# A fused recurrent and expert kernel: the experts' input turned and evicted by halves of the tokens, with scan units and LayerNorm steps moved between the stages

## The chip, the cores and the metric

One core of one Trainium2 chip. The metric is the device time of the whole kernel in microseconds. The kernel before was run three times: 2276.2 us is the median, 2268.3 the lowest and 2276.84 the highest. The kernel is written by engine: each of PE (TensorE), DVE (VectorE), ACT (ScalarE), POOL (GpSimd) and SP (which issues DMAs here) has its own list of instructions, and they meet at semaphores that the program counts itself.

## The reference, cut to what matters

```
x  = L0_attn_h                                  # (8, 512, 256)
xn = layernorm(x)
s  = minGRU-like scan over xn (two layers);  g = silu(expert layer of xn)
x  = x + s * g                                  # first half: phases a and b of the kernel
xn = layernorm(x)
s  = recurrent(xn)      # r,k,v,g,w from low-rank blends; state[i,j] = w[i]*state[i,j] + k[i]*v[j]; y = r . state
                        # 16 heads of 16 x 16; then LayerNorm over the head (ln_w, ln_b), * silu(g), @ oW.T
g  = silu(transformer block of xn):
        h   = xn + attention(rmsnorm(xn))       # 16 heads, latent kv of 32, rope on 32, causal
        hn  = rmsnorm(h) * w_ln2
        out = h + shared_expert(hn) + top-2 of 8 experts(hn)   # down(silu(gate) * up)
x  = x + s * g
```

The change touches the second half only (`phase_c`), which runs once for each of the 8 sequences of 512 tokens. All data are f32.

## The kernel before

`phase_c` (L963) takes the sequences one after another. Each engine runs `before_attention(0)`, `attention(0)`, and then seven times `experts(b)`, `before_attention(b + 1, b)`, `attention(b + 1)`, and at last `experts(7)`.

- **before_attention** (PE L1318, ACT L1552, DVE L1817, POOL L2060): the LoRA products `la_*` and `lb_*`; DVE blends them (L1821) into the mixes, to which POOL adds xn (L2064); projections `pr_*`; the turned input of attention; `ckv` and `q0` to `q7`. DVE's `rotate` (L1848) and POOL (L2079, L2082) apply rope. `sp0`, `sp1` give the bonus term, `lat` the latent values in token order (copied by ACT, L1578). The last steps of the sequence before (`ended`: LayerNorm of the second half of the heads, output product, residual) are woven in.
- **attention** (PE L1383, ACT L1580, DVE L1884, POOL L2084): 32 steps of one query tile and one pair of heads. Per step: `scores` on PE (L1238, L1241), row maximum on DVE (L1777), exp on ACT (L1587), `turn_probs` on PE (L1255), copy on ACT (L1596), and in every second group of four steps `weigh_values` (L1292). At its end the row normalization, the output product by tiles of 128 tokens (`wo0` to `wo3`, L1388), `add_rows` (L1908), `norm_rows` (L1914, L1917).
- **experts** (PE L1426, ACT L1637, DVE L1929, POOL L2105): the 512 normalized rows are turned (L1435), scaled and evicted (`xc0` by DVE, L1927; `xc1` by ACT, L1546), the routing product `gate` (128x8 pieces of L1375), top-two selection on DVE (L1941 to L1971), then nine experts in a row: `up` (two products of 128x512), silu on ACT, `hidden` on DVE (L1977), `down` (128x256 pieces), and DVE's weighted accumulation (L2011). The next sequence's head (L1683 to L1721, up to its `lerp`) is woven in by `between` (L1979).

The **scan units** run beside all this: the recurrence is done in `UNITS` = 32 units per sequence. For unit n SP brings broadcast values (`copy_value`), DVE does `outer(n)` (L1790) and `scan(n)` (L1797), POOL multiplies by r (`product`, L2058), and PE adds up four units (`reduce_state`, L1265) into bank 4 (`whole`). `AHEAD` = 4 units are scanned before attention's first step, those up to `STEPPED` = 22 are spread over the steps by `parts_by_step`, those up to `EARLY` = 24 follow in attention's tail, the rest stand in `experts`. There are 4 state buffers and 6 of products, so a scan waits for the product of four units before, and from the seventh on a product waits for a reduction. `read_out(b, m)` (L1807) takes the sum of 16 units; `mean_last`, `center_last` (L1743), POOL's square (L2116), `var_last` (L1307) and `root_last` (L1550) are the LayerNorm of the second half.

The order of work is written out by hand. `PRE` and `POST` name PE's outputs in order with the engine that reads each; `PRE_BANKS` and `POST_BANKS` give each one of seven PSUM banks, and before PE writes one it waits for the reader of the last output in that bank (`begin`, L1155). The semaphores count in the order of these tables.

## Time and profile before

| what | value |
|---|---|
| median of three runs | 2276.2 us |
| the profiled execution | 2276.78 us, span 2275.0 us from first to last instruction |
| mean granted TensorE clock | 0.963 of 2.4 GHz |
| busy, share of the span | PE 91%, DVE 79%, ACT 43%, POOL 37% |
| `phase_c` | from about 567 us to the end, eight sequences |
| DMA | 66 GB/s over the span |

Times in timelines are us from the span's start. A row of a timeline gives start, duration, engine, line, operation, output and input shapes and the number of merged instructions, and in brackets the engine's idle time before it with what ended it. An f32 product appears as two matmul records.

### The profile page before, as it was taken

Reading aid. Unit: us, or ns where it says so; the run is one execution under the profiler, and the core shown is the slowest. Engines: PE = TensorE matmul, PEld = TensorE weight load, DVE = VectorE, ACT = ScalarE, POOL = GpSimd, SP = SyncE. Lnnn points to the kernel's source line nnn. Section 1 sums busy time; section 2 is a strip of 40 time slices with the busy share of each in tenths; the row PEclk is TensorE's granted clock in tenths of the full one; section 3 lists DMA queues with packets and bytes.
Section 4 is the critical chain, followed back from the end, with each engine's and each line's share of the span. In section 5 each row is a group of like instructions: output and inputs, shape, how many; then the busy total and the mean of one; then the engine's idle time right before and its main releaser. Section 6 shows DMA issues by size and latency. Waiting matters only on the chain.

```text
span 2275.0 us, 37286 instructions
## 1 busy us (share of the span) xinstructions
PE 2062.7 (91%) x11722; PEld 1243.2 (55%) x11723; DVE 1794.2 (79%) x2906; ACT 974.1 (43%) x2556; POOL 846.5 (37%) x666
## 2 busy tenths in 40 slices
PE   7998599997988999998999889998989998899887
PEld 4554599997445445544554455455445544554554
DVE  5997466664697889779897988898798879887985
ACT  3444244442274237334623652373347235612741
POOL 1335200001543364336435542643364346326430
PEclk9999799998999999999999999999999999999998
DMA  6554411113222022211211230222122112302210
GB/s 174 145 158 138 146 54 54 52 55 116 64 57 80 1 65 71 61 37 47 66 47 47 61 86 4 61 66 70 29 56 66 47 47 57 79 15 60 61 48 10
DMA packets 145727, 151.18 MB, mean 66 GB/s; under 512 B 47664, under 2 KB 105648, under 8 KB 145584
## 3 DMA queue, kind: packets, MB, share of 16 engines
q1 hardware_dynamic: 138288, 136.73, 22.0%
q0 software_dynamic: 3072, 8.41, 1.1%
q10 hardware_dynamic: 4224, 4.19, 0.6%
q8 instruction: 83, 1.36, 0.3%
q14 instruction: 60, 0.49, 0.1%
HBM read 121.71 MB, written 27.43 MB: 66 GB/s over the span
## 4 chain that ended last, share of the span: by engine, by line
issue 24%; PE 23%; DVE 18%; POOL 8%; ACT 2%; DMA 0%; POOLq 0%; DVEq 0%; ACTq 0%
PE bank L1375 8%; PE bank L1238 4%; DVE arena L1777 4%; POOL arena L2064 3%; PE bank L1292 3%; DVE arena L1797 3%; DVE arena L1790 3%; PE bank L1255 3%; PE bank L1388 2%; POOL arena L2058 2%; DVE arena L2011 1%; ACT arena L1587 1%; POOL arena L2079 1%; PE bank L1265 1%; DVE arena L1852 1%
## 5 line engine op out<-in xcount | busy, mean ns | idle before, releaser
L2058 POOL TENSOR_TENSOR arena<-arena 128x512 f32<-128x512 f32 x256 | 337.1, 1319 | 567.9 <-DVE arena L1797 491.5
L1375 PE MATMUL bank<-arena 128*128 128x512 f32 (+2 forms) x1312 | 438.6, 489 | 6.8 <-DVE arena L1927 6.8
L1171 PE MATMUL bank<-arena 128*128 128x512 f32 (+2 forms) x768 | 360.5, 614 | 6.8 <-ACT arena L1542 5.4
L1797 DVE TENSOR_TENSOR_SCAN arena<-arena 128x512 f32<-128x512 f32 x256 | 361.9, 1414 | 1.7
L1587 ACT ACTIVATE arena<-bank,arena 128x128 f32<-128x128 f32 (+3 forms) x512 | 266.3, 531 | 194.9 <-DVE arena L1777 193.8
L1375 PEld LDWEIGHTS bank<-arena 128*128 128x128 f32 x1312 | 249.9, 203 | 177.2 <-issue 142.1
L1790 DVE TENSOR_TENSOR arena<-arena 128x512 f32<-128x512 f32 x256 | 249.0, 973 | 40.6 <-DMA arena<-values 36.5
L1238 PE MATMUL bank<-arena 64*128 64x128 f32 (+3 forms) x1024 | 207.5, 481 | 71.4 <-ACT arena L1587 49.7
L1171 PEld LDWEIGHTS bank<-arena 128*128 128x128 f32 (+2 forms) x768 | 139.5, 190 | 198.7 <-issue 171.5
L1777 DVE TENSOR_REDUCE arena<-bank 128x2 f32<-128x256 f32 (+3 forms) x256 | 206.9, 808 | 39.0 <-PE bank L1241 39.0
L1596 ACT ACTIVATE arena<-bank 128x128 f32<-128x128 f32 (+3 forms) x512 | 196.4, 441 | 72.3 <-PE bank L1255 72.3
L1255 PE MATMUL bank<-arena 128*128 128x128 f32 x1280 | 189.1, 278 | 11.3 <-DVE arena L1852 10.7
L283 PE MATMUL bank<-arena 128*128 128x512 f32 x384 | 175.8, 613 | 0.4 <-ACT arena L354 0.4
L1238 PEld LDWEIGHTS bank<-arena 64*128 64x128 f32 x1024 | 77.8, 184 | 154.7 <-issue 59.5
L1255 PEld LDWEIGHTS bank<-arena 128*128 128x128 f32 x1280 | 136.2, 141 | 38.1 <-issue 18.9
L2082 POOL TENSOR_TENSOR arena<-arena 128x512 f32<-128x512 f32 x72 | 112.5, 1562 | 116.0 <-DVE arena L1855 112.8
L691 PE MATMUL bank<-arena 128*128 128x128 f32 x1248 | 148.2, 277 | 5.1 <-DVE arena L791 4.1
L691 PEld LDWEIGHTS bank<-arena 128*128 128x128 f32 x1248 | 147.7, 194 | 7.6 <-issue 4.4
L1546 ACT ACTIVATE arena<-bank 128x512 f32<-128x512 f32 x72 | 42.5, 594 | 253.2 <-PE bank L1375 253.2
L700 PE MATMUL bank<-arena 128*128 x624 | 141.1, 379 | 0.1
L1542 ACT ACTIVATE arena<-bank 128x512 f32<-128x512 f32 (+1 forms) x96 | 57.2, 596 | 194.8 <-PE bank L1171 194.7
L2064 POOL TENSOR_TENSOR arena<-arena 128x512 f32<-128x512 f32 x80 | 102.5, 1307 | 89.1 <-DVE arena L1821 88.5
(200 smaller groups left out, 2960.8 us busy)
## 6 DMA issues: line engine op xcount, KB each, us to landing
arena<-values SPq DMA_DIRECT2D x256, 256.0 KB, 3.4
arena<-in_L_attn_h SPq DMA_DIRECT2D x16, 512.0 KB, 10.4
arena<-in_W1T SPq DMA_DIRECT2D x8, 1024.0 KB
arena<-in_W2T SPq DMA_DIRECT2D x8, 1024.0 KB
sorted_rows<-arena SPq DMA_DIRECT2D x42, 128.5 KB, 9.9
...
```

The lines of the kernel that those rows point to most:

```text
L283: last = nc.tensor.matmul(bank[3 * (n % 2) + q][:, :], gru_w[layer][:, k, q * D + m * P:q * D + (m + 1) * P], source(b, u)[:, k, :], start ...
L691: last = nc.tensor.matmul(zT_bank[u % 2][half][:, (f % 4) * P:(f % 4 + 1) * P], w1_now[u % 2][:, c, f * P:(f + 1) * P], nT[u % 2][:, c, :] ...
L1171: last = nc.tensor.matmul(dst[rows, :], w, x, start=(n == 0), stop=(n == len(pairs) - 1))
L1238: nc.tensor.matmul(bank[2 * (i % LAG) + half][:, 0:n], qT[rows, p, qt * P:(qt + 1) * P], ckvT[rows, 0:n], start=True, stop=False)
L1255: last = nc.tensor.transpose(bank[5 + half][:, kt * P:(kt + 1) * P], probs[s % PROBS][:, kt * P:(kt + 1) * P], ident)
L1375: last = nc.tensor.matmul(dst[o], w, x, start=first, stop=last_one)
L1587: nc.scalar.activation(probs[s % PROBS][:, 0:n], bank[2 * (i % LAG) + half][:, 0:n], ACT.Exp, bias=neg_max[:, s:s + 1], accum_out=row_sum[ ...
L1596: nc.scalar.activation(turned[h % HGROUP][:, 0:qt + 1, qt * P:(qt + 1) * P], bank[5 + half][:, 0:(qt + 1) * P].rearrange("p (k c) -> p k c ...
L1777: nc.vector.tensor_reduce(neg_max[:, 2 * i:2 * i + 2], psum[:, at:at + 1024].rearrange("p (h k) -> p h k", h=2)[:, :, 0:n], X, ALU.max, ne ...
L1790: nc.vector.tensor_tensor(kv[n % 2], copies[n % COPIES], proj["k"][:, n // HD, :], ALU.mult).then_inc(kv_done, 1)
L1797: nc.vector.tensor_tensor_scan(state[n % STATES][:, 1:T + 1], proj["w"][:, m, :], kv[n % 2], VEC["init"][:, m * HD + j:m * HD + j + 1], AL ...
L2058: nc.gpsimd.tensor_tensor(prods[(n + 2) % PRODS], state[n % STATES][:, 0:T], proj["r"][:, m, :], ALU.mult).then_inc(prod_done, 1)
```

## The change

- `AHEAD`, `STEPPED` and `EARLY` are 2, 20 and 22 (they were 4, 22 and 24). Two units leave `before_attention`, and two more stand in `experts`. The reduction of units 16 to 19 moves from attention's end to behind the first transposes of the experts' input.
- The experts' input `xc0`, `xc1` becomes `xc00`, `xc01`, `xc10`, `xc11`: turned and evicted by halves of 256 tokens. `gate` and the first expert's `g0`, `u0` are made in the same halves.
- `wo0` and `wo1` are finished before `wo2` and `wo3` start. `scan(EARLY)` stands behind the second eviction.
- `mean_last`, `center_last`, the square and `var_last` move into the next sequence's `before_attention`, and behind everything for the last sequence. `read_out(b, 1)` moves to the last expert.
- `lat` is made behind q7, `turn_probs` stands before `weigh_values`, the r and g blends before `ln_inv` and `ln_scale`. The wait for SP's load of the next sequence stays at unit 28. Banks are dealt anew.

The diff, cut to its core:

```diff
-EARLY = 24
-STEPPED = 22
-AHEAD = 4
+EARLY = 22
+STEPPED = 20
+AHEAD = 2
...
-QKV = "sp0 sp1 lat q2 q3 q4 q5 q6 q7".split()
+QKV = "sp0 sp1 q2 q3 q4 q5 q6 q7 lat".split()
...
-POST = ([("mean0", "v"), ("wo0", "v"), ("wo1", "v"), ("var0", "a"), ("wo2", "v"), ("wo3", "v"), ("xc0", "v"), ("xc1", "a"),
-         ("gate", "v")]
+POST = ([("mean0", "v"), ("wo0", "v"), ("wo1", "v"), ("wo2", "v"), ("wo3", "v"), ("xc00", "v"), ("xc01", "a"),
+         ("var0", "a"), ("xc10", "v"), ("xc11", "a"), ("gate", "v")]
...
-PRE_BANKS = ([6, 7, 3, 5, 0, 1, 2] + 5 * [3, 5, 6, 7, 0, 1, 2])[:len(PRE)]
-POST_BANKS = (7 * [0, 1, 2, 3, 5, 6, 7])[:len(POST)]
+PRE_BANKS = ([3, 1, 2, 5, 6, 7, 0] + 5 * [3, 5, 6, 7, 0, 1, 2])[:len(PRE) - 7] + [0, 1, 2, 3, 5, 6, 7]
+POST_BANKS = ([0, 1, 2, 5, 6, 7, 0, 3, 1, 2, 5] + 6 * [6, 7, 0, 3, 1, 2, 5])[:len(POST)]
@@ SP, sequence
-                    if n == EARLY + COPIES and not last:
+                    if n == 28 and not last:
@@ PE, before_attention
                 lora_a("rg", 2, 2)
+                if ended is not None:
+                    mean_last(ended)
...
                 lora_b(b, "d", "d", th[2])
+                if ended is not None:
+                    var_last(ended)
                 lora_pair(b, "r", "g", th[1])
@@ PE, attention
                     if i == PSTEPS + 1:
+                        pe.wait_ge(y_out, GROUPS * b + GROUPS - 1)
+                        wo(0, early)
                         pe.wait_ge(y_read, 2 * b + 1)
                         result(b, "mean0", [(full, mean_m, y[:, 0, :], True, True)], bank[post.bank("mean0")])
-                        pe.wait_ge(y_out, GROUPS * b + GROUPS - 1)
-                        wo(0, early)
                         turn_probs(b, i - LAG)
-                    if i == PSTEPS:
-                        reduce_state(b, STEPPED // 4 - 1)
+                    if i < PSTEPS + 1:
+                        turn_probs(b, i - LAG)
                     done = i - LAG - 1
                     if done >= 0 and done % GSTEPS >= NT:
                         weigh_values(b, done // GSTEPS, done % NT)
-                    if i < PSTEPS + 1:
-                        turn_probs(b, i - LAG)
...
                 spread_inverse(b, GROUPS - 1)
-                for i in range(1, NT):
-                    wo(i, early)
+                wo(1, early)
                 pe.wait_ge(y_out, GROUPS * b + GROUPS)
                 wo(0, [GROUPS - 1])
                 wo(1, [GROUPS - 1]).then_inc(made2, 2)
-                pe.wait_ge(sq_done, 2 * b + 1)
-                result(b, "var0", [(full, mean_m, sq[0], True, True)], bank[post.bank("var0")])
+                wo(2, early)
+                wo(3, early)
@@ PE, experts
+                def turn_rows(half):
+                    for k in range(KD):
+                        begin(b, f"xc{half}{k}", post, post_read)
+                    pe.wait_ge(xc_done, 2 * b + half + 1)
+                    for k in range(KD):
+                        for i in (2 * half, 2 * half + 1):
+                            last = nc.tensor.transpose(bank[post.bank(f"xc{half}{k}")][:, (i % 2) * P:(i % 2 + 1) * P],
+                                                       xb[:, i, k * P:(k + 1) * P], ident)
+                    last.then_inc(made2, 2)
+
+                def gate_tiles(half):
+                    dst = bank[post.bank("gate")]
+                    for i in (2 * half, 2 * half + 1):
+                        for k in range(KD):
+                            last = nc.tensor.matmul(dst[:, i * ME:(i + 1) * ME], xbT[:, k, i * P:(i + 1) * P], gate_w[:, k, :],
+                                                    start=(k == 0), stop=(k == KD - 1))
+                    return last
+
+                def up_half(name, w, half):
+                    cols = slice(2 * P * half, 2 * P * (half + 1))
+                    for k in range(KD):
+                        last = nc.tensor.matmul(bank[post.bank(name)][:, cols], w[:, k, :], xbT[:, k, cols],
+                                                start=(k == 0), stop=(k == KD - 1))
+                    return last
+
+                turn_rows(0)
+                reduce_state(b, STEPPED // 4 - 1)
+                pe.wait_ge(sq_done, 2 * b + 1)
+                result(b, "var0", [(full, mean_m, sq[0], True, True)], bank[post.bank("var0")])
+                pe.wait_ge(v_read2, post.read(b, "xc00"))
+                pe.wait_ge(a_read2, post.read(b, "xc01"))
+                pe.wait_ge(moe_in, 16 * 3 * (ME + 1))
+                begin(b, "gate", post, post_read)
+                gate_tiles(0)
+                first = (("g0", eg_w[0]), ("u0", eu_w[0]))
+                for name, w in first:
+                    begin(b, name, post, post_read)
+                    up_half(name, w, 0)
+                turn_rows(1)
+                pe.wait_ge(v_read2, post.read(b, "xc10"))
+                pe.wait_ge(a_read2, post.read(b, "xc11"))
+                gate_tiles(1).then_inc(made2, 1)
+                for name, w in first:
+                    up_half(name, w, 1).then_inc(made2, 1)
...
-                    if e == 2:
-                        reduce_state(b, EARLY // 4)
-                    elif e == 6:
-                        reduce_state(b, EARLY // 4 + 1)
-                    elif e == ME:
-                        mean_last(b)
+                    for at, g in ((2, 5), (4, 6), (ME, 7)):
+                        if e == at:
+                            reduce_state(b, g)
                     if e:
                         down(e - 1)
-                var_last(b)
@@ ACT, attention (and bring_rows(1) in the place of xc1)
+                def bring_rows(half):
+                    act.wait_ge(made2, post.made(b, f"xc{half}1"))
+                    cols = slice(2 * P * half, 2 * P * (half + 1))
+                    nc.scalar.activation(xbT[:, 1, cols], bank[post.bank(f"xc{half}1")][:, 0:2 * P], ACT.Copy,
+                                         scale=VEC["w_ln2"][:, 1:2]).then_inc(a_read2, 1)
...
+                    if half == 0:
+                        bring_rows(0)
@@ DVE, before_attention
+                if ended is not None:
+                    center_last(ended)
-                for name in ("v0", "k0", "v1", "k1", "d0", "d1"):
+                for name in ("v0", "k0", "v1", "k1", "d0", "d1", "r0", "g0", "r1", "g1"):
...
-                outer(b, 3)
...
-                scan(b, 2)
...
-                    if name == "q2":
-                        unit(b, AHEAD - 1)
@@ DVE, attention
                 add_rows(0)
                 outer(b, EARLY)
                 norm_rows(0)
...
                 add_rows(1)
+                bring_rows(0)
+                norm_rows(1)
+                bring_rows(1)
                 scan(b, EARLY)
-                norm_rows(1)
@@ DVE, experts
-                    if e < 4:
+                    if e < 6:
                         unit(b, EARLY + 4 + e)
-                    elif e == 5:
-                        read_out(b, 1)
+                    elif e == 6:
                         ln_inv(b, 0)
-                    elif e == 6:
+                    elif e == 7:
                         ln_scale(b, 0)
-                    elif e == 7:
-                        center_last(b)
                     elif e == 8:
                         ln_gate(b, 0)
+                        read_out(b, 1)
@@ POOL
-            def before_attention(b):
+            def before_attention(b, ended):
+                if ended is not None:
+                    square_last(ended)
...
-                    elif n == 3:
-                        product(b, 2)
-                        product(b, 3)
...
+                    if n == UNITS - 2 and not final:
+                        head_rstd(b + 1)
                     product(b, n)
```

## Rows read from the trace of the kernel before

**Rows 1.** The page, busy time of the engines, whole span.

```profile
PE 2062.7 (91%) x11722; PEld 1243.2 (55%) x11723; DVE 1794.2 (79%) x2906; ACT 974.1 (43%) x2556; POOL 846.5 (37%) x666
```

**Rows 2.** Busy time by stretch: window; length, busy us (instructions) of PE, PEld, DVE, ACT, POOL; PEclk, DMA share, GB/s.

```profile
916.20:1128.00 211.80, 194.39 (x1129) 106.86 (x1128) 178.99 (x255) 93.49 (x263) 92.31 (x69) 0.97 0.20 53
...
1128.00:1335.70 207.70, 190.20 (x1129) 104.09 (x1129) 178.20 (x255) 93.30 (x263) 93.42 (x69) 0.99 0.21 54
```

**Rows 3.** One line's instructions: `center`, with duration min/median/max, first and last start.

```profile
L1887 DVE TENSOR_TENSOR arena<-arena,bank x8: 686/689/689, 704.0 to 2179.3; 128x512 f32<-128x512 f32 x8
```

**Rows 4.** Busy time by stretch, short windows, columns as above.

```profile
933.00:943.00 10.00, 9.15 (x26) 5.76 (x25) 8.87 (x19) 3.19 (x5) 4.82 (x6) 0.51 0.46 112
...
1147.60:1151.10 3.50, 3.50 (x6) 1.53 (x6) 3.46 (x5) 0.57 (x2) 2.00 (x2) 0.51 0.56 150
...
553.70:577.60 23.90, 19.80 (x79) 16.14 (x80) 9.86 (x23) 6.29 (x23) 2.06 (x2) 0.50 0.53 150
```

**Rows 5.** Timeline of PE, tail of attention and start of the experts.

```profile
1132.89 4.91 PE L1388 MATMUL bank<-arena 128*128 128x256 f32 x22
...
1140.87 0.63 PE L1435 MATMUL bank<-arena 128*128 128x128 f32 x4 [1.35 <-DVE arena L1917]
...
1141.43 1.07 PE L1265 MATMUL bank<-arena 128*32 128x512 f32 x8
...
1144.33 0.66 PE L1435 MATMUL bank<-arena 128*128 128x128 f32 x4 [1.83 <-DVE arena L1917]
...
1145.83 15.86 PE L1375 MATMUL bank<-arena 128*128 128x8 f32 x48 [0.84 <-DVE arena L1927]
```

**Rows 6.** Timeline of DVE, same stretch.

```profile
1137.91 0.69 DVE L1908 TENSOR_TENSOR arena<-arena,bank 128x512 f32<-128x512 f32 x1 [2.94 <-PE bank L1388]
...
1145.03 0.75 DVE L1927 TENSOR_SCALAR arena<-bank,arena 128x512 f32<-128x512 f32 x1 [0.75 <-PE bank L1435]
...
1145.69 0.68 DVE L1790 TENSOR_TENSOR arena<-arena 128x512 f32<-128x512 f32 x1
...
1155.52 0.69 DVE L1977 TENSOR_TENSOR arena<-arena,bank 128x512 f32<-128x512 f32 x1
```

**Rows 7.** Timeline of DVE, late experts.

```profile
1185.99 1.74 DVE L2011 SCALAR_TENSOR_TENSOR arena<-bank,arena 128x256 f32<-128x256 f32 x4 [1.30 <-PE bank L1375]
...
1196.40 0.69 DVE L1977 TENSOR_TENSOR arena<-arena,bank 128x512 f32<-128x512 f32 x1 [1.89 <-PE bank L1375]
...
1201.63 2.08 DVE L1721 SCALAR_TENSOR_TENSOR arena<-arena 128x512 f32<-128x512 f32 x2
```

**Rows 8.** Timeline of PE, end of the experts.

```profile
1196.99 3.62 PE L1375 MATMUL bank<-arena 128*128 128x256 f32 x16
...
1202.54 1.13 PE L1307 MATMUL bank<-arena 128*128 128x512 f32 x2 [1.94 <-POOL arena L2116]
```

**Rows 9.** Timeline of PE, queries and first scores.

```profile
1244.84 1.07 PE L1363 MATMUL bank<-arena 32*128 32x32 f32 x8
...
1245.84 7.14 PE L1171 MATMUL bank<-arena 128*128 128x512 f32 x16
...
1258.07 0.70 PE L1238 MATMUL bank<-arena 64*128 64x256 f32 x4 [2.02 <-DVE arena L1852]
```

**Rows 10.** Timeline of DVE, before attention.

```profile
1239.63 1.66 DVE L1790 TENSOR_TENSOR arena<-arena 128x512 f32<-128x512 f32 x1
...
1243.43 2.29 DVE L1797 TENSOR_TENSOR_SCAN arena<-arena 128x512 f32<-128x512 f32 x1
...
1246.83 1.27 DVE L1797 TENSOR_TENSOR_SCAN arena<-arena 128x512 f32<-128x512 f32 x1
...
1248.02 1.69 DVE L1790 TENSOR_TENSOR arena<-arena 128x512 f32<-128x512 f32 x1
```

**Rows 11.** Timeline of POOL, before attention.

```profile
1249.12 2.58 POOL L2058 TENSOR_TENSOR arena<-arena 128x512 f32<-128x512 f32 x2
```

**Rows 12.** Timelines of DVE and PE, end of the run.

```profile
2251.54 1.41 DVE L2011 SCALAR_TENSOR_TENSOR arena<-bank,arena 128x256 f32<-128x256 f32 x4
...
2252.80 1.13 PE L1307 MATMUL bank<-arena 128*128 128x512 f32 x2 [0.95 <-POOL arena L2116]
```

53 lines of the change are left out of this document (25 added, 28 removed).

## The prediction

> **What bounds the kernel now.** I read the page first [rows 1]: PE is busy 91% of the span. That average says "PE", so the second view was busy time by stretch, cut from one `center` (L1887) to the next, one cycle per sequence [rows 2]. Two things show. A cycle has 190.2 us of PE time and 178.2 us of DVE time in 207.7 us, so both rest, but at different places. And cycles come in two lengths, 207.7 and 211.8; the long one has the lower mean clock (0.97 against 0.99) and 4.2 us more PE time for the same 1129 records. From the first `center` to the last [rows 3] there are (2179.3 - 704.0) / 7 = 210.8 us per cycle, so most are long.
>
> Short windows [rows 4] say where: behind the pauses of PE in the row normalization the granted clock is 0.51, the lower level of 1.2 GHz, for all of 933 to 943 in the long cycle, and only from 1147.6 to 1151.1 in the short one.
>
> Then the timelines of the short cycle. At the **end of attention** PE turns the normalized rows and pauses three times, 1.35, 1.83 and 0.84 us [rows 5]. But DVE [rows 6] goes with no pause over 0.3 us from `bring` (1145.03) through scans and the top-two routing to `hidden(0)` at 1155.52, and PE's first `down` product started right behind that. What an earlier PE meets is therefore DVE. In the **late experts** DVE rests (1.30, 1.89) [rows 7], and PE waits 1.94 for POOL's square before `var_last` [rows 8]. At the **start of attention** PE waits up to 2.02 for a rotation by DVE [rows 9]; in DVE's queue ahead of the rotations stand `outer`/`scan` of 1.66, 2.29, 1.27 and 1.69 us [rows 10].
>
> **The change, part by part**, for one cycle, in the short one's times.
>
> 1. *AHEAD 4 to 2.* DVE loses two units ahead of the rotations: 1.66 + 2.29 + 1.27 + 1.69 = 6.9 us [rows 10], POOL two products, 2.58 the pair beside them [rows 11]. The rotation of q2 starts behind them, at 1249.6. Its product was ready at 1247.6 (four of the sixteen records from 1245.84 on, 7.14 us together), and `lat`, 1.0 us from 1244.84, moves from before it to behind q7 [rows 9]. From there to the last rotation DVE has the work of before, so the gain is 2.0 (slack of q2) + 1.0 (lat) = 3.0 us. The rest of the 6.9 only becomes DVE idle time.
>
> 2. *The same two units land in the experts*, in `between(4)` and `between(5)`: a scan 1.27 [rows 10] and an outer 0.68 [rows 6] each, 3.9 us; at the price beside a busy POOL, 2.29 + 1.66 [rows 10], 7.9. I take 3.9: POOL has little work then. From `hidden(0)` to the end of the lerp DVE needs 1203.7 - 1155.5 = 48.2 us. Less the idle 3.2 [rows 7], plus 3.9, less `center_last` and `read_out(1)` (0.68 each) that now come later: 47.5. The lerp, for which the next sequence's LoRA products wait, ends at 1203.0, 0.7 sooner than now (at the dear price 3.3 later). That is DVE's floor.
>
> 3. *mean_last and var_last behind the LoRA products.* The wait of 1.94 [rows 8] goes. Both matmuls stay, at 7.14 / 16 x 2 = 0.9 us [rows 9]: in the experts another `reduce_state` (1.07) [rows 5] stands for mean_last, and the LoRA stretch gets both: +1.8. From the products' start (-0.7) to q2: +1.1. Queued behind: `center_last` is now ahead of DVE's blends, but its matmul comes before theirs; POOL's square, 2.0 us, is ahead of its first mix, which `project v` wants four PE groups later. Nothing for either.
>
> 4. *The halves.* Of the 22 records of output products [rows 5] that stood ahead of `add_rows(0)` 10 remain, 12 x 0.21 = 2.6 us less, so it runs at 1135.3 and not at 1137.91 [rows 6]. PE then has work without a pause: wo2/3, transposes, reduction, var0, half a gate, the half up products. By my layout `norm_rows(1)` ends on DVE at 1141.9, PE comes to the second transposes at 1143.3 and DVE's second `bring_rows` ends at 1144.45. But the scan that stood between the norms (1.27) now follows it, so the next `outer` starts at 1144.45 + 1.2 = 1145.7; it started at 1145.69 [rows 6]. The DVE idle time (2.94, 0.75) is moved, not removed. **`hidden(0)` stays at 1155.5.** PE has ended up(0) and up(1) at 1150.6 and waits 5.6 us. The halves alone turn three short PE pauses into a long one.
>
> 5. *Clock.* Behind pauses of 4 us in a stretch of seven the clock was low for 10 us or for 3.5 [rows 4]. Behind 5.6 us in one piece I expect the same, 6.8 as the middle. It now falls on `down(0)` and what follows and costs PE half of itself: the experts' products end at 1200.6 [rows 8] + 3.4 = 1204.0, 1.0 behind DVE's floor. The Trainium skill (TensorE: Matmul & The Clock Gate, "HAM oscillation") has it that a long pause in every pass of a loop pays for the cold clock in every pass; taken alone, the rule speaks against this change, in all eight sequences. The rows agree with it for the old pauses; none shows one of 5.6 us.
>
> 6. *Small moves.* One `reduce_state` (1.07) leaves the end of attention, where PE's last products are what DVE waits for, and `turn_probs` goes before `weigh_values`. Bounds 0 and 3 us (both, and once more for the order); I take 1.5, since the next scores stand behind the two in either order. The next sequence's loads are issued some 9 us later, behind `outer(24)`; wanted at 1167.5, there by about 1160: hidden; without that cover DVE would wait in `head_gate`.
>
> **Sum of a cycle**: 207.7 - 1.5 (part 6) - 3.0 (1) + 1.1 (2, 3) + 1.0 (5) = 205.3. Seven cycles of 210.8 become 205.3: -38.5. The first sequence, ahead of the first `center`, gains part 1 without much else: -2.5. At the **end of the run** nothing covers mean, centre, square and variance: the last accumulation ends at 2252.95, + 0.75 + 0.68 + 1.03 + 0.68 + 1.04 + 1.13 = 2258.3 where var_last ended at 2253.9 [rows 12]: +4. The profiled execution of 2276.8 becomes 2239.8. It is 0.6 above the median shown, 2276.2: **2239**.
>
> **Rivals.**
> - *The long pause costs more clock and part 6 gives nothing* (0.20). By the sum a cycle is 201.9 + half of the low-clock time. At 10 us it is 206.9, without part 6 208.4: 2276.8 - 7 x 2.4 + 1.5 = 2262. For: most cycles had the 10 us. Against: DVE's floor hides part.
> - *The halves do bring the routing forward* (0.15). If the second `bring_rows` isn't held by the half up products (1.7 us) DVE gains 2 us and the pause is too short to lower the clock: the LoRA products start at 1201.0, the cycle is 202.3: 2276.8 - 59.5 + 1.5 = 2219.
> - *Nothing to measure* (0.09). POOL's adds, not the units, hold the rotations [rows 11], so part 1 gives nothing, nor does part 6: 207.7 + 1.1 + 1.0 = 209.8, 2276.8 - 7 + 4 = 2274.
> - *Slower* (0.06). The pause before `down(0)` leaves PE at its low level for long; by the same sum 210.8 is reached at 18 us of it. For: there is a stretch of 24 us, 553.7 to 577.6 [rows 4], at the change of phase. At 24 us a cycle is 213.9: 2276.8 + 22 + 1.5 = 2300. Against: once fed, PE is dense for 45 us here.
> - The forecast, with 3.5 to 8 us of low clock: 0.50.
>
> **Numbers.** A measurement of this kernel tells some 0.5% (11 us) from no change. Faster by more, under 2265: the forecast and the first two rivals: 0.85. Within: 0.09. Slower: 0.06. The range takes in the first rival's 2262 and most of the second's 2219, and with it both ends of part 6 (10 us either way): 2214 to 2262.
>
> **What would show it.** Right: no PE pause over 0.5 us before the first transposes of the experts' input, but one of 4 to 6 us before the first 256-column product of the experts, ended by `hidden(0)`, and the low clock just behind; no 2 us pause at the first scores; DVE without idle from the second `bring_rows` to the late experts; even cycles of 203 to 207. Wrong: less than 19 us from `add_rows(0)` to `hidden(0)` (20.2 by part 4); scores still waiting for a rotation (1); PE waiting over 2 us for the lerp (2); DVE waiting for a DMA in `head_gate` (6).

## The result: 2260.12 us, 15 us faster, and the profile after

| | before | after |
|---|---|---|
| median, us | 2275.11 (six runs) | 2260.12 (six runs, 2258.26 to 2260.59) |
| ratio | | 0.994 [0.9926, 0.9953] |
| profiled execution; span, us | 2276.78; 2275.0 | 2260.01; 2258.2 |
| mean granted clock | 0.963 | 0.961 |
| first `center`, us | 704.0 | 700.4 |
| mean cycle (first to last `center`, by 7), us | 210.8 | 207.9 |
| last `center` to the end of the span, us | 95.6 | 102.6 |

Faster, as forecast, but by 15 us and not by 37: 2260 lies inside the range and 21 us above the predicted 2239. The three lower lines say where. A cycle gained 2.9 us (205.3 was predicted, 207.9 came), the first sequence 3.6, and the end of the run lost 7.0: -20.3 - 3.6 + 7.0 = -16.9 us of span. Of the 21 us that are missing, 18 are missing in the cycles.

The page of the changed kernel, its engines' busy time, to be read against [rows 1]:

```profile
PE 2040.5 (90%) x11786; PEld 1247.4 (55%) x11787; DVE 1770.9 (78%) x2914; ACT 979.1 (43%) x2564; POOL 826.2 (37%) x666
```

The one line of `center`, which is L1919 now, against [rows 3]:

```profile
L1919 DVE TENSOR_TENSOR arena<-arena,bank x8: 686/687/689, 700.4 to 2155.5; 128x512 f32<-128x512 f32 x8
```

Busy time by stretch: first two whole cycles, cut at `center` as in [rows 2], then short windows as in [rows 4] (columns as there):

```profile
906.50:1116.60 210.10, 192.18 (x1139) 107.42 (x1138) 176.15 (x257) 94.18 (x263) 89.31 (x69) 0.97 0.20 53
1116.60:1322.80 206.20, 187.95 (x1139) 105.38 (x1138) 176.20 (x257) 93.91 (x263) 89.52 (x69) 0.98 0.21 55
...
932.70:939.40 6.70, 5.11 (x10) 3.53 (x11) 4.18 (x12) 0.92 (x2) 2.13 (x3) 0.50 0.48 125
984.00:987.00 3.00, 3.00 (x4) 1.18 (x4) 2.27 (x6) 1.06 (x1) 0.00 (x0) 0.50 0.01 3
1049.00:1052.00 3.00, 3.00 (x16) 2.20 (x14) 1.97 (x3) 1.88 (x7) 1.09 (x1) 0.50 0.24 81
1140.90:1147.70 6.80, 3.32 (x8) 2.67 (x9) 4.27 (x17) 1.18 (x3) 3.72 (x4) 0.50 0.76 226
```

Both cycles lost DVE time (176.2 against some 178.5), and both gained on their counterparts. But there are still two lengths, now strictly in turn: 206.1, 210.1, 206.2, 210.1, 206.3, 210.1, 206.3. The short windows show the granted clock at its lower level, 1.2 GHz: 6.7 to 6.8 us of it in each cycle, and 3.4 us more twice in each long one, at the LoRA products and at the start of attention (seen here in 984.0 to 987.0 and 1049.0 to 1052.0). PE was busy for 5.11 us of the first window and for only 3.32 of the one of the short cycle.

Timeline of PE in the short cycle, end of attention to the LoRA products, against [rows 5, 8]:

```profile
1120.15 5.78 PE L1392 MATMUL bank<-arena 128*128 128x256 f32 x26
1125.76 0.60 PE L1434 MATMUL bank<-arena 128*128 128x128 f32 x4
...
1129.06 1.98 PE L1449 MATMUL bank<-arena 128*128 128x256 f32 x8
1130.88 0.60 PE L1434 MATMUL bank<-arena 128*128 128x128 f32 x4
...
1134.83 3.60 PE L1379 MATMUL bank<-arena 128*128 128x512 f32 x8
1144.38 7.05 PE L1379 MATMUL bank<-arena 128*128 128x256 f32 x16 [5.95 <-DVE arena L2014]
...
1186.62 3.73 PE L1379 MATMUL bank<-arena 128*128 128x256 f32 x16
1192.89 3.71 PE L1171 MATMUL bank<-arena 128*128 128x512 f32 x8 [2.55 <-DVE arena L1758]
```

The first transposes (1125.76), the reduction, var0, the half gate and the half up products run on without a pause, as laid out. `down(0)` starts at 1144.38 behind a pause of 5.95 us that `hidden(0)` ends, where 5.6 was predicted, and the window 1140.9 to 1147.7 lies across it. At the other end the LoRA products start 2.55 us behind PE's last product of the experts.

Timeline of DVE, same stretch, against [rows 6, 7]:

```profile
1126.64 0.48 DVE L1958 TENSOR_SCALAR arena<-bank,arena 128x256 f32<-128x256 f32 x1
...
1131.51 0.48 DVE L1958 TENSOR_SCALAR arena<-bank,arena 128x256 f32<-128x256 f32 x1 [2.67 <-PE bank L1434]
1131.91 1.28 DVE L1834 TENSOR_TENSOR_SCAN arena<-arena 128x512 f32<-128x512 f32 x1
...
1133.81 1.99 DVE L1834 TENSOR_TENSOR_SCAN arena<-arena 128x512 f32<-128x512 f32 x1
...
1136.42 2.00 DVE L1834 TENSOR_TENSOR_SCAN arena<-arena 128x512 f32<-128x512 f32 x1
...
1143.63 1.28 DVE L2014 TENSOR_TENSOR arena<-arena,bank 128x512 f32<-128x512 f32 x2
...
1187.79 1.74 DVE L2046 SCALAR_TENSOR_TENSOR arena<-bank,arena 128x256 f32<-128x256 f32 x4 [0.75 <-PE bank L1379]
...
1191.42 1.42 DVE L1758 SCALAR_TENSOR_TENSOR arena<-arena 128x512 f32<-128x512 f32 x2
```

DVE sits idle for 2.67 us before the second `bring_rows` (L1958): PE does half an up and half a gate product (L1449, 1129.06) before the second transposes (1130.88). The scan right behind takes 1.28 us and the next two 1.99 and 2.00. `hidden(0)` is the row at 1143.63. From `scale_values` of the last group (1120.35) that is 23.3 us; it was 22.4 before in the short cycles and 22.9 in the long ones.

Start of attention, timeline of DVE, for part 1, and of PE below it; against [rows 9]:

```profile
1237.92 0.69 DVE L1887 TENSOR_TENSOR arena<-bank,arena 128x512 f32<-128x512 f32 x1 [1.03 <-PE bank L1171]
```

```profile
1230.84 12.20 PE L1171 MATMUL bank<-arena 128*128 128x512 f32 x28
...
1245.81 0.70 PE L1238 MATMUL bank<-arena 64*128 64x256 f32 x4 [0.36 <-DVE arena L1888]
```

The rotation of q2 (1237.92) now waits for PE (1.03), where PE waited for it, and the pause at the first scores fell from 2.02 to 0.36.

### The profile page after: what moved, and what is told of

It is laid out like the page before. It is cut to its first block, busy times and chain, and to the rows that moved or that the text cites. A ratio compares the mean times of both kernels' runs of the same rounds, so it can differ in the third digit from the quotient of the medians.

```text
span 2258.2 us, 37446 instructions
## 1 busy us (share of the span) xinstructions
PE 2040.5 (90%) x11786; PEld 1247.4 (55%) x11787; DVE 1770.9 (78%) x2914; ACT 979.1 (43%) x2564; POOL 826.2 (37%) x666
## 3 DMA queue, kind: packets, MB, share of 16 engines
q1 hardware_dynamic: 138288, 136.73, 22.4%
## 4 chain that ended last, share of the span: by engine, by line
PE 27%; issue 22%; DVE 17%; POOL 7%; ACT 3%; DMA 0%; POOLq 0%; DVEq 0%; ACTq 0%
PE bank L1238 5%; PE bank L1379 5%; PE bank L1255 4%; PE bank L1292 3%; DVE arena L1827 3%; POOL arena L2104 3%; DVE arena L1834 3%; PE bank L1392 3%; DVE arena L1814 2%; DVE arena L2046 2%; ACT arena L1612 2%; PE bank L1171 2%; PE bank L1241 1%; PE bank L1265 1%; POOL arena L2096 1%
## 5 line engine op out<-in xcount | busy, mean ns | idle before, releaser
L2096 POOL TENSOR_TENSOR arena<-arena 128x512 f32<-128x512 f32 x256 | 344.0, 1345 | 607.7 <-DVE arena L1834 574.8
L1379 PE MATMUL bank<-arena 128*128 128x256 f32 (+1 forms) x1120 | 390.0, 503 | 47.4 <-DVE arena L2014 47.4
L1171 PE MATMUL bank<-arena 128*128 128x512 f32 (+2 forms) x768 | 356.4, 611 | 24.3 <-DVE arena L1758 17.8
L1834 DVE TENSOR_TENSOR_SCAN arena<-arena 128x512 f32<-128x512 f32 x256 | 355.6, 1389 | 1.7
L1379 PEld LDWEIGHTS bank<-arena 128*128 128x128 f32 x1120 | 218.8, 199 | 207.1 <-issue 128.0
L1827 DVE TENSOR_TENSOR arena<-arena 128x512 f32<-128x512 f32 x256 | 241.4, 943 | 40.9 <-DMA arena<-values 36.6
L2119 POOL TENSOR_TENSOR arena<-arena 128x512 f32<-128x512 f32 x72 | 98.0, 1361 | 155.5 <-DVE arena L1891 152.4
L691 PEld LDWEIGHTS bank<-arena 128*128 128x128 f32 x1248 | 147.8, 194 | 7.6 <-issue 4.4
L1255 PEld LDWEIGHTS bank<-arena 128*128 128x128 f32 x1280 | 139.2, 143 | 19.1 <-ACT arena L1612 10.8
L2046 DVE SCALAR_TENSOR_TENSOR arena<-bank,arena 128x256 f32<-128x256 f32 x288 | 120.0, 469 | 32.3 <-PE bank L1379 32.0
```

Source lines behind the costliest of these rows:

```text
L691: last = nc.tensor.matmul(zT_bank[u % 2][half][:, (f % 4) * P:(f % 4 + 1) * P], w1_now[u % 2][:, c, f * P:(f + 1) * P], nT[u % 2][:, c, :] ...
L1171: last = nc.tensor.matmul(dst[rows, :], w, x, start=(n == 0), stop=(n == len(pairs) - 1))
L1255: last = nc.tensor.transpose(bank[5 + half][:, kt * P:(kt + 1) * P], probs[s % PROBS][:, kt * P:(kt + 1) * P], ident)
L1379: last = nc.tensor.matmul(dst[o], w, x, start=first, stop=last_one)
L1827: nc.vector.tensor_tensor(kv[n % 2], copies[n % COPIES], proj["k"][:, n // HD, :], ALU.mult).then_inc(kv_done, 1)
L1834: nc.vector.tensor_tensor_scan(state[n % STATES][:, 1:T + 1], proj["w"][:, m, :], kv[n % 2], VEC["init"][:, m * HD + j:m * HD + j + 1], AL ...
```

## The experiments

Twelve kernels ran, in three groups; each is given by its ratio to the kernel before on the same chip in the same group (medians of before 2271.0, 2271.1 and 2272.4). "Offset" is the time from `scale_values` of the last group, the last thing that all the versions have alike, in the same short cycle. For the changed kernel: `hidden(0)` 23.3, end of PE's expert products 70.0, LoRA products 72.55 (73.5 in the long cycles), rotation of q2 117.6, next `scale_values` 206.2. For the kernel before: 22.4, 67.5, 70.7, 116.5, 207.7. The edits are against the changed kernel. Its own ratio of 0.994 would be 2257 in these groups, where it was not run again; so what an experiment gains on it is the difference of medians or up to 3 us less. One more caution: ahead of the first `center` the changed kernel and the experiments other than 2 and 7 run the same instructions, and still their profiled executions reach it at anything from 694.7 to 700.8 us. None of that is an edit's doing; the mean cycle and the end of the run are what an edit sets. So the 3.6 us by which the first `center` came sooner than before (704.0) can't be put down to the change with any certainty either. Kernels of the experiments stand beside one another directly.

### 1. Only the place of scan(EARLY)

```diff
@@ DVE, attention
                 norm_rows(1)
-                bring_rows(1)
                 scan(b, EARLY)
+                bring_rows(1)
```

> The changed kernel with one line moved: DVE's scan(EARLY) stands ahead of the second bring_rows again, in DVE's idle 2.67 us there. Theory A (DVE is the bound from add_rows to hidden(0)): hidden(0) comes 1.2 us sooner (22.1 us behind the start of scale_values instead of 23.3) and PE's pause before down(0) shrinks from 5.95 to about 4.7; if DVE also sets the lerp, the cycle shortens by 1.2, seven cycles by 8 us: 2252. Theory B (the halves' time is set by PE or by its clock behind the pause): hidden(0) sooner, but the start of the LoRA products stays within 0.3 us and the kernel within 3 us of 2260.

Measured: **2239.45, ratio 0.986 [0.984, 0.9882]**. One line swapped brings more than the whole change did. DVE in this kernel:

```profile
1125.01 0.48 DVE L1958 TENSOR_SCALAR arena<-bank,arena 128x256 f32<-128x256 f32 x1 [1.48 <-PE bank L1434]
...
1128.04 2.00 DVE L1834 TENSOR_TENSOR_SCAN arena<-arena 128x512 f32<-128x512 f32 x1
...
1135.25 1.28 DVE L2014 TENSOR_TENSOR arena<-arena,bank 128x512 f32<-128x512 f32 x2
```

The idle time is 1.48 and not 2.67, since the scan stands in it. `hidden(0)` comes at offset 21.4, 1.9 sooner: 1.2 from the filled idle time, 0.7 because only one scan (1128.04, 2.00) and not two (1133.81 and 1136.42 in the changed kernel) takes 2.0 us, as beside a POOL product. The pause before `down(0)` is 4.06, its low clock 3.4 us and not 6.8 in six of seven cycles. LoRA products at 70.7, mean cycle 205.2. Theory A had the direction right; its 1.2 us and 2252 were too little. The sum of the prediction had given this away: in part 4 I placed the scan behind the norms by the diff, wrote down that this costs its duration, and then counted the idle time as "moved".

### 2. The units back ahead of the rotations

```diff
-EARLY = 22
-STEPPED = 20
-AHEAD = 2
+EARLY = 24
+STEPPED = 22
+AHEAD = 4
...
@@ DVE, before_attention
                 rotate(2)
+                outer(b, 3)
...
+                scan(b, 2)
...
+                    if name == "q2":
+                        unit(b, AHEAD - 1)
```

> The changed kernel with AHEAD, STEPPED and EARLY back at 4, 22 and 24, and so two units ahead of the rotations again and two fewer in the experts; all else as changed. Theory A (the units cost in the experts what they bring at attention's start): the start of the LoRA products is 3 to 4 us sooner, the rotation of q2 starts 3 us later behind them, and the kernel is within 6 us of 2260. Theory B (moving them is the one part of the change that gains): slower than the changed kernel by 3 us in each of eight sequences, 2284. Theory C (it is the part that loses): 2240.

Measured: **2303.85, ratio 1.0135 [1.0096, 1.0173]**, mean cycle 213.8. From LoRA products to the rotation of q2 it is 48.0 us against 45.0: +3.0, part 1's term. From there to `center` it is 1.5 us more in the last three cycles and 3.4 to 3.6 in the first three. Theory B, 2284, had the sign and the 3 us of part 1; another 20 us came on top. The experts gave nothing back, though DVE had two units less to do there: the LoRA products start at 73.2 to 74.7, not sooner. PE waits once for DVE (1.07), early; the wait behind PE's last product is what it was:

```profile
1184.22 15.80 PE L1379 MATMUL bank<-arena 128*128 128x256 f32 x48 [1.07 <-DVE arena L2018]
...
1213.27 1.99 PE L1171 MATMUL bank<-arena 128*128 128x512 f32 x4 [2.55 <-DVE arena L1758]
```

So the two units in the experts cost nothing, and the LoRA start isn't DVE's floor. Why the first three cycles (214.6 to 214.8) are 3 us longer than the last three (211.6 to 211.7) stays open: both have 10.2 us of low clock each. The fourth, 217.7, has 17. Part of it is where the queries begin: in the first four PE waits 1.8 and 2.0 us for two rotations, in the last three 1.8 and 0.6.

### 3. PE filled ahead of the LoRA products

Three products whose result nothing reads are added ahead of the wait for the lerp.

```diff
@@ PE, before_attention
+                if ended is not None:
+                    begin(b, "la_vk", pre, pre_read)
+                    for _ in range(3):
+                        nc.tensor.matmul(bank[pre.bank("la_vk")][:, :], ident, xbT[:, 0, :], start=True, stop=True)
                 pe.wait_ge(lerp_done, b + 1)
```

> The changed kernel, and PE does three 128x512 products (2.6 us) that nobody reads, ahead of its wait for the lerp, where it pauses for 2.55 us in every cycle. Nothing else changes and no work is moved. Theory A (this pause brings the low clock at the LoRA products in every second cycle, and with it the 3.9 us by which those cycles are longer): all cycles take 206.2 us and the kernel is 3 x 3.9 = 12 us faster than the changed one, 2248. Theory B (the low clock there comes from the pauses of attention or from elsewhere): cycles keep their two lengths, 2260.

Measured: **2246.56, ratio 0.9887 [0.9866, 0.9908]**, theory A (2248). The granted clock around the LoRA products:

```profile
979.00:990.00 11.00, 11.00 (x32) 4.62 (x31) 8.51 (x16) 2.14 (x3) 2.00 (x2) 1.00 0.00 1
```

In the same place of the changed kernel the row 984.00 stands at 0.50. No cycle has low clock at the LoRA products or at the start of attention any more; the cycles are nearly even (206.0 to 207.7, mean 206.9). The long cycles lost 2.9 of their extra 3.9 us for 2.6 us of useless PE work. The first `center` comes 2.0 sooner, which the edit can't have done, as it touches nothing ahead of it; behind it the profiled execution is 8.8 us shorter. So in the changed kernel the low clock at the LoRA products hangs on the pause of 2.55 us, though it falls there only in every second cycle. With it went the low clock at the start of attention, which nothing was filled for.

### 4. PE filled ahead of down(0)

Six unread products ahead of the wait for `hidden(0)`.

```diff
@@ PE, experts
                 def down(e):
+                    if e == 0:
+                        begin(b, "d0a", post, post_read)
+                        for _ in range(6):
+                            nc.tensor.matmul(bank[post.bank("d0a")][:, :], ident, xbT[:, 0, :], start=True, stop=True)
                     pe.wait_ge(hid_done
```

> The changed kernel, and PE does six 128x512 products (5.2 us) that nobody reads, in its pause of 5.95 us before down(0). Theory A (DVE sets the time to the lerp, and the low clock behind the pause only costs the 2.2 us for which DVE waits on the first down products): no low clock at down(0), the LoRA products start about 2 us sooner in each of seven cycles, 2246. Theory B (the low clock of 6.8 us there costs half of itself on the path, as predicted): 3.4 us a cycle, 2236. Theory C (it costs nothing, the lerp hides it): 2260.

Measured: **2239.15, ratio 0.986 [0.9838, 0.9882]**, between the theories. PE's timeline:

```profile
1128.92 5.31 PE L1482 MATMUL bank<-arena 128*128 128x512 f32 x12
1135.03 5.43 PE L1379 MATMUL bank<-arena 128*128 128x256 f32 x16 [0.79 <-DVE arena L2018]
```

`down(0)` starts at offset 24.0 as in the changed kernel, and nothing of it is low. The experts' products then last 44.4 us; they last 46.0 in a short cycle of the changed kernel and 47.0 in a long one. So 6.8 us of low clock cost 1.6 us there and 2.6 in a long cycle. That is half of what PE does in the window (3.32 and 5.11 us, halves 1.65 and 2.55), and the rest of the window is pause. Most of what this kernel gained beyond that (mean cycle 205.4, the end 97.5) is the low clock that no longer follows later: only four 3.4-us stretches are left between 960 and 2200 us.

### 5. The halves undone

`turn_rows(1)` stands ahead of the gate product, with only the reduction and var0 between it and `turn_rows(0)`; then the gate product whole and `up(0)` whole; the scan between the norms, both `bring_rows` behind, on DVE and on ACT. What stays in two pieces are the transposes and their evictions, so this is the order of before and not its instructions.

```diff
@@ PE, experts
                 result(b, "var0", ...)
+                turn_rows(1)
...
                 gate_tiles(0)
-                    up_half(name, w, 0)
-                turn_rows(1)
...
-                    up_half(name, w, 1).then_inc(made2, 1)
...
-                    if 0 < e <= ME:
+                    if e <= ME:
                         up(e)
@@ DVE, attention
                 add_rows(1)
-                bring_rows(0)
+                scan(b, EARLY)
                 norm_rows(1)
+                bring_rows(0)
                 bring_rows(1)
-                scan(b, EARLY)
```

> The changed kernel with the halves undone: both transposes are evicted after the second norm, gate and up(0) are whole again behind them, and scan(EARLY) stands between the norms, as before the change. Theory A (the halves bring nothing, since DVE reaches hidden(0) no sooner): hidden(0) within 1 us of 23.3 us behind scale_values, PE's pause before down(0) is gone or under 3 us, cycles within 2 us of 207.9, kernel 2248 to 2262. Theory B (the halves are what gained): slower than the changed kernel by 2 us a cycle, 2276. Theory C (with scan(EARLY) in its old place hidden(0) is 1 to 2 us sooner and the whole is faster than the changed kernel, because what the halves part did was to move that scan): 2245 or less.

Measured: **2227.52, ratio 0.9819 [0.9797, 0.984]**, theory C. The change without the halves' order brings 2271.1 - 2227.5 = 44 us, and the halves with their order give some 30 of it back. `hidden(0)` stands at offset 20.3, 3.0 sooner, mean cycle 204.5, the end 96.3 against 102.6. PE pauses where it did before, only shorter, and the clock still falls in six of the seven cycles, for 6.8 us in five of them and for 3.4 in one (PE's timeline, then the window behind):

```profile
1323.81 0.63 PE L1434 MATMUL bank<-arena 128*128 128x128 f32 x4 [1.31 <-DVE arena L1940]
1325.05 2.35 PE L1442 MATMUL bank<-arena 128*128 128x8 f32 x16 [0.61 <-DVE arena L1949]
1327.25 13.09 PE L1379 MATMUL bank<-arena 128*128 128x512 f32 x27
```

```profile
1326.40:1333.20 6.80, 6.80 (x13) 3.35 (x13) 6.39 (x16) 1.01 (x2) 4.45 (x6) 0.50 0.59 182
```

### 6. LayerNorm steps back at the end of the experts

```diff
@@ PE, before_attention
-                if ended is not None:
-                    mean_last(ended)
...
-                if ended is not None:
-                    var_last(ended)
@@ PE, experts
+                    if e == ME:
+                        mean_last(b)
                     if e:
                         down(e - 1)
+                    if e == ME - 1:
+                        reduce_state(b, 7)
+                var_last(b)
```

with `center_last`, the square and `read_out(b, 1)` back in their old places on DVE and POOL.

> The changed kernel with the LayerNorm of the second half back in the experts (mean_last ahead of the last down products, center_last in between(7), the square and var_last at the end; the last reduction one expert sooner so that this can be), all else as changed. Theory A (moving it took PE's wait for the square away and put two products in a stretch that PE fills, so it is about even in the cycle and dear at the run's end): PE waits about 2 us before var_last again, the stretch from the LoRA products to the rotation of q2 is 1.8 to 2.1 us shorter, the end of the run some 6 us shorter; 2250 to 2262. Theory B (the move gained what the measured 15 us are): 2272 or more.

Measured: **2253.08, ratio 0.9927 [0.9907, 0.9947]**. The mean cycle is 208.1, and all are alike (207.9 to 208.2): 0.2 more than the mean of the changed kernel. Two pauses of PE stand there in place of one, and the clock is low behind them in every cycle and not in every second:

```profile
1187.29 1.13 PE L1307 MATMUL bank<-arena 128*128 128x512 f32 x2 [1.39 <-POOL arena L2153]
1189.89 5.40 PE L1171 MATMUL bank<-arena 128*128 128x512 f32 x8 [1.47 <-DVE arena L1757]
```

The end of the run is 4.2 shorter (98.4 against 102.6). The first `center` is 5.1 sooner, ahead of all that was edited. So, as theory A had it, the move is worth about nothing in the cycle and costs some 4 us at the end.

### 7. weigh_values before turn_probs

```diff
@@ PE, attention
-                    if i < PSTEPS + 1:
-                        turn_probs(b, i - LAG)
                     done = i - LAG - 1
                     if done >= 0 and done % GSTEPS >= NT:
                         weigh_values(b, done // GSTEPS, done % NT)
+                    if i < PSTEPS + 1:
+                        turn_probs(b, i - LAG)
```

> The changed kernel with weigh_values ahead of turn_probs again. Theory A (the order gains a little in attention): rotation of q7 to center 0.5 to 1 us longer in each cycle, kernel 4 to 8 us slower than the changed one, 2265. Theory B (the next scores stand behind both anyway): within 3 us of 2260. Theory C (it costs): faster by over 3 us.

Measured in ten runs: 2263.7 (2258.4 to 2275.2), ratio 0.9975 [0.9954, 0.9995]. From the last rotation to `center` 74.5 us against 73.2: the order is worth 1.3 us of a short cycle (207.4 against 206.2), most of part 6. The long cycles don't show it (209.4 to 210.6), as they have no low clock at the start of attention here; so the mean is 208.5 against 207.9 and the whole run 4 us longer, which is theory A.

### 8. hidden(0) and hidden(1) ahead of the routing

Experiment 1, and the two `hidden` ahead of the top-two selection on DVE, their silus ahead of the routing's `tanh` on ACT.

```diff
@@ DVE, experts
                 unit(b, EARLY + 1)
+                hidden(0)
                 unit(b, EARLY + 2)
+                hidden(1)
...
-                hidden(0)
                 for e in range(ME + 1):
-                    if e < ME:
+                    if 0 < e < ME:
                         hidden(e + 1)
@@ ACT, experts
+                take2(b, "g0", silu_g[0], ACT.Silu).then_inc(a_read2, 1)
+                take2(b, "g1", silu_g[1], ACT.Silu).then_inc(a_read2, 1)
                 act.wait_ge(comb_in, 2 * b + 2)
                 nc.scalar.activation(routs[4], routs[4], ACT.Tanh, scale=0.5).then_inc(comb_out, 1)
-                take2(b, "g0", silu_g[0], ACT.Silu).then_inc(a_read2, 1)
-                take2(b, "g1", silu_g[1], ACT.Silu).then_inc(a_read2, 1)
```

> scan(EARLY) ahead of the second bring_rows as in e1_scan_first, and DVE does hidden(0) and hidden(1) between and behind the two units ahead of the routing, ACT the first two silus ahead of its tanh, so that PE need not wait for the routing with its first down products. Theory A (PE from down(0) on sets when the lerp comes: a dense 44.4 us, then a fixed 2.55): the long pause and its low clock go, and the LoRA products start up to 4 us sooner than in e1_scan_first: 2239 - 28 = 2211. Theory B (DVE's own work from the second bring_rows to the lerp is the floor, as the prediction had it): the LoRA products start no more than 1 us sooner than in e1_scan_first, PE has new pauses in the middle of the experts, 2232 to 2242.

Measured: **2202.45, ratio 0.9707 [0.9687, 0.9726]**, the fastest of all, 69 us under the kernel before. PE's timeline and the granted clock in it:

```profile
1114.76 1.03 PE L1442 MATMUL bank<-arena 128*128 128x8 f32 x8 [0.66 <-DVE arena L1958]
...
1117.45 8.77 PE L1379 MATMUL bank<-arena 128*128 128x512 f32 x24
```

```profile
1110.00:1125.00 15.00, 14.34 (x60) 9.78 (x61) 10.55 (x27) 5.61 (x12) 6.92 (x8) 1.00 0.48 130
```

`hidden(0)` is at offset 14.75, ahead of PE's need. PE has one pause of 0.66 in the whole passage and the clock stays at its full level. The LoRA products start at 65.3 in five cycles and at 67.3 in two (why isn't known), behind a pause of 2.8 to 2.9 us that has low clock behind it in five. The mean cycle is 201.2 and the end 93.3. It is theory A, and 9 us better than its 2211.

### 9. The same with whole products

Experiment 5 with experiment 8's order of the `hidden`.

> e5_no_halves with hidden(0) and hidden(1) ahead of the routing, as in e8_hidden_early. Theory A (the two gains add, since one ends DVE's way to the routing sooner and the other takes PE's wait for it away): cycles near 200, kernel 2190 to 2200. Theory B (with the waits of PE gone, PE's dense work from up(0) on sets the LoRA products, and the whole up products start later than the halves did): 2202 or slower, as in e8_hidden_early.

Measured: **2227.74, ratio 0.98 [0.9782, 0.9817]**, theory B: no better than experiment 5. Timelines of PE and DVE and two windows:

```profile
1325.43 0.63 PE L1434 MATMUL bank<-arena 128*128 128x128 f32 x4 [1.31 <-DVE arena L1940]
...
1328.45 13.98 PE L1379 MATMUL bank<-arena 128*128 128x512 f32 x32
```

```profile
1333.93 0.69 DVE L1961 TENSOR_TENSOR arena<-arena,bank 128x512 f32<-128x512 f32 x1 [4.85 <-PE bank L1379]
```

```profile
1329.70:1333.10 3.40, 3.40 (x5) 1.35 (x4) 0.00 (x0) 0.60 (x1) 0.33 (x1) 0.50 0.59 115
1121.40:1128.20 6.80, 6.80 (x18) 4.22 (x18) 1.73 (x2) 2.26 (x4) 1.37 (x1) 0.50 0.60 155
```

Now DVE waits 4.85 us, for `up(0)`, and part of `up(0)` runs at 1.2 GHz, behind the pauses of 1.31 and 0.61. `hidden(0)` comes at offset 17.85 in the cycles with 3.4 us of low clock there and at 19.55 in those with 6.8.

Experiments 1, 5, 8 and 9 are a square:

| | routing before `hidden(0)` | `hidden(0)` before routing |
|---|---|---|
| whole | 2227.5 | 2227.7 |
| halves, scan ahead of `bring_rows(1)` | 2239.5 | 2202.5 |

With DVE's routing in the way the halves cost 12 us, without it they gain 25. Neither edit does anything good alone. The four stand on three chips, each compared with the kernel before on its own; the ratios (0.9819, 0.98, 0.986, 0.9707) say the same.

### 10. The second transposes ahead of the half up products

```diff
@@ PE, experts
+                turn_rows(1)
                 for name, w in first:
                     begin(b, name, post, post_read)
                     up_half(name, w, 0)
-                turn_rows(1)
```

> The changed kernel with PE's second transposes moved ahead of the half up products (behind the first half of gate); halves, banks and scan(EARLY) as changed. Theory A (in e5_no_halves hidden(0) came 3.0 us sooner because nothing stood on PE in front of the second transposes, 1.1 us, and because scan(EARLY) was not behind the eviction, 1.9 us): the second bring_rows is about 1.8 us sooner, hidden(0) 1.1 to 1.8 us sooner (21.5 to 22.2 us behind scale_values), the LoRA products as much, kernel 2244 to 2252. Theory B (the halves cost by their number of instructions and banks, not by order): hidden(0) within 0.4 us of 23.3 and the kernel within 4 us of 2260.

Measured: **2239.42, ratio 0.985 [0.9831, 0.9869]**, theory A, though 5 us under its range. DVE's wait before the second `bring_rows`:

```profile
1121.59 0.48 DVE L1958 TENSOR_SCALAR arena<-bank,arena 128x256 f32<-128x256 f32 x1 [0.89 <-PE bank L1434]
```

0.89 and not 2.67, so `hidden(0)` comes at 21.5, 1.8 sooner, nearly as in experiment 1: two ways to the same 20 us. It settles what the wait was for. The mean cycle is 206.1, though, against 205.2 there, and behind the first `center` the two profiled executions gain 16 and 22 us. The two edits in one kernel, which should leave little of the halves' 3.0 us, were not run.

### 11 and 12. On experiment 9: the last sequence's LayerNorm in the experts; the filling

Experiment 11 takes experiment 9 and, for the last sequence alone, `mean_last`, `center_last` and `var_last` at the end of the experts:

```diff
@@ PE, experts
+                    if final and e == ME:
+                        mean_last(b)
...
+                if final:
+                    var_last(b)
```

> e9_whole_early, and for the last sequence alone the LayerNorm of its second half stays inside the experts as before the change. Theory (the move costs 4 to 7 us at the end of the run, where nothing covers it): 4 to 6 us less from the last center to the end than in e9_whole_early, cycles the same. Rival (the end is set by the low clock of the last products): within 2 us of it.

Measured: 2223.4, ratio 0.9773 [0.9755, 0.9792], 4.3 under experiment 9 at the medians. From the last `center` to the end 92.2 against 96.6, with the same mean cycle (204.5): the 4.4 us that the move costs at the end, theory A.

Experiment 12 takes experiment 9 and experiment 3's three unread products, with the same edit as there.

> e9_whole_early with the three unread products of e3_fill_lora ahead of the wait for the lerp. Theory A (PE's pause there still brings the low clock into some cycles, at 1.6 to 2 us each): 3 to 8 us faster than e9_whole_early. Theory B (without the long pause at down(0) the one of 2.6 us no longer lowers the clock): within 2 us of it, or slower by the products' drain.

Measured: 2220.45, ratio 0.9765 [0.9736, 0.9793], 7 under experiment 9, though the two intervals overlap; mean cycle 203.5 against 204.5, and no low clock at the LoRA products. It seems to pay here too, by some half of what it paid in experiment 3.

Experiment 8 with 11's end, or with the filling, wasn't tried.

## Why the prediction was right and where it was wrong

The predicted cycle was 205.3 and the mean one 207.9. The 2.6 us, with what each stretch was forecast to do and did:

| stretch | forecast | measured | off by |
|---|---|---|---|
| start of the LoRA products behind `scale_values`, in a short cycle | +0.3 | +1.9 | +1.6 |
| from there to the rotation of q2 (parts 1 and 3) | -1.2 | -0.85 | +0.35 |
| from there to the next `scale_values` (part 6) | -1.5 | -2.55 | -1.05 |
| mean cycle over a short one | 0 | +1.7 | +1.7 |

7 x 2.6 = 18, and 3 us at the end of the run, less 1 at the start, make 20 of the 21 us.

**Two steps of the prediction failed.** The first is the start of the LoRA products, which it took as the later of two times, DVE's own floor (part 2) and the end of PE's products (part 5). The lerp follows PE instead, by 2.55 us. The second is the even cycles (part 5): every second cycle is 3.9 us longer. Each is 1.6 or 1.7 us a cycle, 11 to 12 us in all, where the forecast was 37. The wrong claim of part 4, that `hidden(0)` stays where it was, is 0.9 of the first. A sign of being wrong that was named in advance came: PE waits over 2 us for the lerp (2.55). A sign of being right, even cycles, did not.

- **Part 1, the units (-3.0): right.** From the first rotation to that of q2 the measured gain is 3.0, and experiment 2 gives the 3.0 back. DVE waits for q2's product now, as the slack of 2.0 said.
- **Part 2, the units in the experts (3.9 us of DVE work): right that they are hidden, wrong in what I set against them. This is the first step that failed.** I took the end of the lerp as a floor of DVE's own, at 1203.0 of the old time axis, with PE free to be up to 1.0 later. It is no floor. The accumulation of the eighth expert, `ln_scale` and the lerp follow PE's `down(7)`, as the two rows 1187.79 and 1191.42 show, so the LoRA products start 2.55 us behind PE's last product. They do so in every cycle of the changed kernel and of experiments 1, 2, 4, 5, 7 and 10 (2.8 to 2.9 in 8, 9 and 11), wherever PE ends between offsets 65.4 and 72.2, and also with two units less (experiment 2). What delays PE by a microsecond delays the next sequence by one. PE itself ended at 70.0, where the sum has 70.9: `hidden(0)` was 0.9 late, the low clock 1.8 cheaper than its 3.4. With the 2.55 behind it, the LoRA start came 1.9 later than before where I had +0.3: +1.6 per cycle. The rows of before had it: PE's last expert product ends at 1200.6 [rows 8] and the lerp at 1203.7 [rows 7], 3.1 behind, of which `center_last` is 0.68. There `var_last` and its wait lay over it; part 3 counted that wait as gone, and a longer one took its place.
- **Part 3, mean_last and var_last (+1.8 in the LoRA stretch): right**; it measured +2.1. The price at the end of the run was +4 and experiments 6 and 11 say 4.2 and 4.4.
- **Part 4, the halves: short by 0.9, and by more in what it didn't ask.** PE's part came as laid out (pause 5.95 against 5.6, the output products first). But "the DVE idle time is moved, not removed; `hidden(0)` stays at 1155.5" was short by 0.9. Of that, 0.7 is a second scan of 2.0 us where there was one: the scan behind the second `bring_rows` has its POOL product beside the next scan. This 0.9 passes on to PE in full. More important, I compared with the kernel before only, where the rest of the change would have brought `hidden(0)` forward by 2.1 (20.3 in experiment 5 against 22.4). The halves' true price is 3.0 us at `hidden(0)`, 3.4 a cycle, some 30 us in all. Had I priced the change without its halves, this would have stood out as a part to doubt.
- **Part 5, the clock: its cost was read off wrongly in both directions. The second is the other step that failed.** Behind the long pause I had 6.8 us of low clock, and 6.7 to 6.8 came, in every cycle. It cost 1.6 to 2.6 us and not 3.4 (experiment 4), since PE can't lose what it isn't doing: part of the window lay in the pause itself. Missed was the other low clock. In three cycles of seven it falls behind the 2.55 us before the LoRA products (1.7 us lost) and again at the start of attention, behind a pause of 1.47 us that the short cycles have too (1.2 lost). The window at `down(0)` costs 1.0 more in the same cycles. They are 3.9 longer, which is 1.7 a cycle in the mean, and experiment 3 takes 2.9 of the 3.9 away. I had expected even cycles, and 3.1 of the 5.5 us per cycle forecast rested on that: the sum started from the short cycle, 207.7, where the mean before was 210.8. Short against short the change gained 1.5 us. The Trainium skill (TensorE: Matmul & The Clock Gate, "HAM oscillation") says that a long pause in each pass of a loop is paid for in each pass; the trace agrees for the pause of 5.95. The same section takes the cost as the throttled time times one half; that would be 3.4 us where 1.6 and 2.6 were measured.
- **Part 6, small moves (-1.5): too little.** From q2 to the next `scale_values` the gain is 2.55, of which the order of `turn_probs` is 1.3 (experiment 7). Both lay within the bounds of 0 and 3. The loads were in time: no wait for a DMA in `head_gate`.
- **The end of the run (+4): 7.0.** Of these 4.7 lie behind PE's last expert product (27.9 us to the end of the span, 23.2 before): the LayerNorm, priced at 4, in which the low clock of its matmuls takes 0.7 + 0.9. The other 2.3 are in the last sequence's experts, with their late `hidden(0)` and their own low clock; I had counted that seven times and not eight. PE and then DVE at the end of the changed kernel, against [rows 12]:

```profile
2227.74 2.54 PE L1379 MATMUL bank<-arena 128*128 128x256 f32 x11
2232.77 1.76 PE L1303 MATMUL bank<-arena 128*128 128x512 f32 x2 [2.49 <-DVE arena L1844]
2236.43 2.08 PE L1307 MATMUL bank<-arena 128*128 128x512 f32 x2 [1.90 <-POOL arena L2157]
2244.25 3.78 PE L1314 MATMUL bank<-arena 128*128 128x256 f32 x8 [5.74 <-DVE arena L1796]
```

```profile
2234.57 0.69 DVE L1780 TENSOR_TENSOR arena<-arena,bank 128x512 f32<-128x512 f32 x1 [1.85 <-PE bank L1303]
2239.27 3.35 DVE L1787 RECIPROCAL arena<-arena 128x512 f32<-128x512 f32 x1 [4.01 <-ACT arena L1578]
```

The mean's two products take 1.76 and the variance's two 2.08, for 1.02 and 1.13 at full clock. The prediction priced them by rows with a busy PE around them.

None of the rivals came by its own mechanism. The first stands 2 us from the measured time with its 2262, and that is luck: the low clock behind the long pause was 6.8 us and not 10, and part 6 gave more than forecast, not nothing. The second, "the halves do bring the routing forward", 2219 at 0.15, named the right place. In the changed kernel the hold on the second `bring_rows` was there (2.67 us); experiment 10 takes it away and gains the 2 us that the rival said (1.8), experiment 1 fills it with the scan and gains 1.9, and either is worth some 20 us in all. Lying inside the range is in part luck too: part 6 and the cheaper low clock made up for some of what the two failed steps cost.

**What stays open**: why the clock falls in every second cycle and not in each when the pauses are the same (behind the pause of 2.55 us it fell in three cycles of seven in the changed kernel, in six in experiment 5, in two in experiment 4 and in one in experiment 2), and why the first cycles of experiment 2 are longer than the last. The runs show where the low stretches fall, not what sets them.
